# An encoder of four layers on one core: half of the second expert product in fp16 halves, the mask and the bias in fewer columns

## The reference

```
wei = jnp.einsum('bhtf,bhsf->bhts', q, k) * d ** (-0.5)
wei = jax.nn.softmax(jnp.where(tril, wei, -jnp.inf), axis=-1)
...
h = jax.nn.relu(jnp.einsum('nd,edf->enf', flat, W1) + b1[:, None, :])
eo = jnp.einsum('enf,efd->end', h, W2) + b2[:, None, :]
moe = jnp.einsum('ne,end->nd', combine, eo)
out = y + layernorm(moe.reshape(b, t, d), ln2_g, ln2_b)
```

## Time and profile before

| | before |
|---|---|
| median of the timed runs | 496.46 us (496.34 to 497.64, 3 runs) |
| the profiled execution | 499.61 us |
| its span | 497.7 us |
| mean granted clock of PE | 0.97 |
| PE busy | 458.0 us, 92% |
| ACT busy | 365.1 us, 73% |
| DVE busy | 306.5 us, 62% |
| POOL busy | 160.0 us, 32% |

### The profile page before, as it was taken

How to read it: one execution, slowest core, us unless ns; L and a number is a source line. 1 busy time by engine, 2 the same in 40 slices (tenths; PEclk the granted TensorE clock), 3 DMA queues, 4 the chain that set the end, 5 groups by cost and what they waited for, 6 DMA issues and landing times.

```text
span 497.7 us, 18273 instructions
## 1 busy us (share of the span) xinstructions
PE 458.0 (92%) x7501; PEld 380.6 (76%) x7501; DVE 306.5 (62%) x941; ACT 365.1 (73%) x906; POOL 160.0 (32%) x400
## 2 busy tenths in 40 slices
PE   6959889888889999999999999999999999999793
PEld 4736566666667888898888888898789788799693
DVE  3588988868778666487874784646634754323211
ACT  4687688788788896977779769776887676665452
POOL 6764241122224432335241144221322221432302
PEclk9778999899989999999999999999999999999997
DMA  7930000000000000000000000000000000000000
GB/s 194 380 116 3 8 3 10 9 3 3 3 3 13 3 13 3 13 3 12 3 13 3 1 3 8 10 1 3 14 3 1 1 13 4 1 12 1 12 1 12
DMA packets 7930, 11.39 MB, mean 23 GB/s; under 512 B 593, under 2 KB 7209, under 8 KB 7465
## 3 DMA queue, kind: packets, MB, share of 16 engines
q1 hardware_dynamic: 7848, 10.23, 6.3%
HBM read 9.18 MB, written 1.05 MB: 21 GB/s over the span
## 4 chain that ended last, share of the span: by engine, by line
PE 76%; DVE 10%; ACT 5%; POOL 4%; issue 3%; SPq 1%; DMA 0%; POOLq 0%; DVEq 0%; ACTq 0%
PE bk L639 23%; PE bk L629 8%; PE bk L689 6%; PE bk L691 5%; PE bk L690 5%; PE bk L615 4%; ACT w1f L806 3%; DVE negmax L1031 3%; PE bk L608 3%; PE bk L585 2%; PE bk L601 2%; PE bk L534 2%; PE bk L488 2%; PE bk L548 1%; PE bk L497 1%
## 5 line engine op out<-in xcount | busy, mean ns | idle before, releaser
L832 ACT ACTIVATE hT<-bk,pk 128x256 f32<-128x256 f32 x256 | 107.8, 479 | 41.3 <-PE bk L691 41.2
L639 PE MATMUL bk<-w2f,hT 128*128 128x128 f32 x1024 | 135.5, 276 | 1.0 <-ACT hT L832 1.0
L639 PEld LDWEIGHTS bk<-w2f,hT 128*128 128x128 f32 x1024 | 124.2, 192 | 3.9 <-ACT hT L832 1.3
L806 ACT ACTIVATE w1f<-bk 128x512 f32<-128x512 f32 (+1 forms) x192 | 98.8, 601 | 24.0 <-PE bk L615 23.4
L1031 DVE TENSOR_REDUCE negmax<-bk 128x4 f32<-128x512 f32 (+1 forms) x192 | 104.9, 612 | 15.9 <-PE bk L615 15.7
L962 DVE SCALAR_TENSOR_TENSOR acc<-bk,comb,acc 128x128 f32<-128x128 f32 x128 | 38.8, 345 | 79.9 <-PE bk L639 79.8
L689 PE MATMUL bk<-yhi,w1hi 128*128 128x256 f16 x256 | 70.2, 274 | 0.0
L691 PE MATMUL bk<-yhi,w1lo 128*128 128x256 f16 x256 | 69.8, 273 | 0.0
L690 PE MATMUL bk<-ylo,w1hi 128*128 128x256 f16 x256 | 69.8, 273 | 0.0
L629 PE MATMUL bk<-w1f,val 128*32 128x128 f32 (+1 forms) x1536 | 51.8, 278 | 2.2 <-ACT w1f L806 2.2
L615 PE MATMUL bk<-qk 32*128 32x128 f16 (+2 forms) x1536 | 46.0, 215 | 8.1 <-DVE negmax L1031 3.6
(11 more groups left out here) (150 smaller groups left out, 781.6 us busy)
## 6 DMA issues: line engine op xcount, KB each, us to landing
w1f<-in_w SPq DMA_DIRECT2D x1, 2048.0 KB, 14.9
w2f<-in_w SPq DMA_DIRECT2D x1, 2048.0 KB
pk<-in_pack SPq DMA_DIRECT2D x1, 1690.0 KB, 8.3
xin<-in_x SPq DMA_DIRECT2D x8, 128.0 KB, 2.3
out<-outb SPq DMA_DIRECT2D x8, 128.0 KB, 1.8
ctxT<-in_turned SPq DMA_DIRECT2D x8, 77.0 KB
cin<-in_ctx SPq DMA_DIRECT2D x8, 77.0 KB
hf<-in_half SPq DMA_DIRECT2D x1, 416.0 KB, 10.5
```

The costliest lines, as they stand in the source:

```text
L639: last = mm(o[:, i * D:(i + 1) * D], hT[:, k % HRING, i * T:(i + 1) * T], w2f[:, k, :], start=c == 0 and i == 0, stop=c == CH - 1, skip_gr ...
L806: act.activation(probs[0:nk, ring(n, q), :], bank(g, st, q)[0:nk, :], ACT.Exp, scale=SCALE[L]).then_inc(s_exp, 1)
L832: act.activation(hT[:, k % HRING, :], bank(g, st)[:, m * W:(m + 1) * W], ACT.Relu, bias=P("b1")[:, k:k + 1]).then_inc(s_relu, 1)
```

## The change

The constants of the mask are laid out anew, so that one product of 32 rows, 128 columns of the array and 128 columns of data writes 32 key columns of four heads for all 128 queries; four such rounds on four row groups make the mask. `combT` holds both samples' weights in 16 rows, made by one transposition, and the bias product is one with 256 columns against a block-diagonal `b2f`.

Every odd unit of the down product becomes three fp16 products of halves for each sample: hi x W2 hi, hi x W2 lo, lo x W2 hi. The halves of W2's odd units are made by four new steps "part" of lane 6 (ACT the high half, DVE the low). The halves of the relu are made by the new step "halve" behind each "moe": DVE copies `hT` into fp16, POOL subtracts (in the last job, `LATE`, DVE subtracts too). The halves lie in the place that W2's odd units had. ACT does the odd unit's relu first. `down` runs two pieces behind the up products instead of one, "moe_end" has four units, `HRING` is 6. `ORDER` and `TAKEN` are written anew throughout; the steps of the five lanes come in nearly the same sequence (on average 1.6 places away), and the pieces stand at about the same places between them.

```
-BANKS, RING, HRING = 8, 8, 4
+BANKS, RING, HRING = 8, 8, 6
...
-        return [("split", lane, n) for n in range(SPLITS)]
+        return [("split", lane, n) for n in range(SPLITS)] + [("part", lane, n) for n in range(PARTED)]
...
-        return ([("moe_start", lane)] + [("moe", lane, n) for n in range(PIECES)]
+        return ([("moe_start", lane)] + [(kind, lane, n) for n in range(PIECES) for kind in ("moe", "halve")]
...
-                    for i in range(SPS):
-                        last = pe.transpose(o[0:E1, i * T:(i + 1) * T], comb[s][:, i, :], ident)
+                    last = pe.transpose(o[0:SPS * E1, 0:T], comb[s][:].rearrange("p i e -> p (i e)"), ident)
...
-                            o = banks[q][32 * c:32 * c + 32, :].rearrange("p (t k) -> p t k", t=NT)
-                            mm(o, H(low)[rows_, :], H(spread)[rows_, x:x + T].unsqueeze(1).to_broadcast((32, NT, T)),
-                               start=True, stop=False)
+                            o = banks[q][:].rearrange("p (t k) -> p t k", t=NT)[:, :, 32 * c:32 * c + 32]
+                            mm(o, H(low)[rows_, x:x + T], H(spread)[rows_, :].unsqueeze(1).to_broadcast((32, NT, 32)),
+                               start=c == 0, stop=False)
...
             def down(j, k):
                 e, c = divmod(k, CH)
-                o = take_bank(pe, j, ("moe", MOE, 2 * e + 1), 1) if c == 0 else products(j, e)
-                pe.wait_ge(s_relu, j * UNITS + k + 1)
+                o = take_bank(pe, j, *emptied(e)) if c == 0 else products(j, e)
+                if k % 2 == 0:
+                    pe.wait_ge(s_relu, j * UNITS + k + 2)
+                    for i in range(SPS):
+                        last = mm(o[:, i * D:(i + 1) * D], hT[:, k % HRING, i * T:(i + 1) * T], w2f[:, k, :],
+                                  start=c == 0 and i == 0, stop=False, skip_group_check=True)
+                    last.then_inc(s_down, 1)
+                    return
+                u = j * ODD + k // 2
+                hi, lo = hhi(u), hlo(u)
+                pe.wait_ge(s_hhi, hi_done(u))
                 for i in range(SPS):
-                    last = mm(o[:, i * D:(i + 1) * D], hT[:, k % HRING, i * T:(i + 1) * T], w2f[:, k, :],
-                              start=c == 0 and i == 0, stop=c == CH - 1, skip_group_check=True)
+                    for w in (w2hi[:, k // 2, :], lo_of_unit(k)):
+                        mm(o[:, i * D:(i + 1) * D], hi[:, i * T:(i + 1) * T], w, start=False, stop=False,
+                           skip_group_check=True)
+                pe.wait_ge(*((s_hhi, hi_done(u) + 1) if j >= LATE else (s_hlo, u + 1)))
+                for i in range(SPS):
+                    last = mm(o[:, i * D:(i + 1) * D], lo[:, i * T:(i + 1) * T], w2hi[:, k // 2, :],
+                              start=False, stop=c == CH - 1, skip_group_check=True)
                 last.then_inc(s_down, 1)
...
-                    for i in range(SPS):
-                        last = mm(o[:, i * D:(i + 1) * D], combT[s][:, i * T:(i + 1) * T], b2f[:],
-                                  start=True, stop=True)
+                    last = mm(o[:, 0:SPS * D], combT[s][:], b2f[:], start=True, stop=True)
...
-                    if n:
-                        down(g, 2 * n - 2)
-                        down(g, 2 * n - 1)
+                    if n > 1:
+                        down(g, 2 * n - 4)
+                        down(g, 2 * n - 3)
                 elif kind == "moe_end":
-                    down(g, UNITS - 2)
-                    down(g, UNITS - 1)
+                    for k in range(UNITS - 4, UNITS):
+                        down(g, k)
...
+                elif kind == "part":
+                    act.wait_ge(s_moe, N_MOE * 16)
+                    act.activation(hi_of_w2(st[2]), odd_of_w2(st[2]), ACT.Copy).then_inc(s_w1hi, 1)
...
-                    for m in range(2):
+                    for m in (1, 0):
...
+                elif kind == "part":
+                    n = st[2]
+                    dve.wait_ge(s_w1hi, SPLITS + n + 1)
+                    dve.wait_ge(s_w1lo, SPLITS + n)
+                    dve.tensor_tensor(lo_of_w2(n), odd_of_w2(n), hi_of_w2(n), ALU.subtract).then_inc(s_w1lo, 1)
+                elif kind == "halve":
+                    k = 2 * st[2] + 1
+                    u = g * ODD + st[2]
+                    dve.wait_ge(s_relu, g * UNITS + k)
+                    dve.tensor_copy(hhi(u), hT[:, k % HRING, :]).then_inc(s_hhi, 1)
+                    if g >= LATE:
+                        dve.wait_ge(s_hhi, hi_done(u))
+                        dve.tensor_tensor(hlo(u), hT[:, k % HRING, :],
+                                          hhi(u), ALU.subtract).then_inc(s_hhi, 1)
...
+                elif kind == "halve" and g < LATE:
+                    k = 2 * st[2] + 1
+                    u = g * ODD + st[2]
+                    pool.wait_ge(s_hhi, u + 1)
+                    pool.tensor_tensor(hlo(u), hT[:, k % HRING, :], hhi(u),
+                                       ALU.subtract).then_inc(s_hlo, 1)
```

More of the change, by code:

```diff
@@ L21 @@
 SPLITS = 8
+PARTED = 4
+ODD = E1 * 2
+LATE = 7
 SPS = 2
@@ L140, in uses @@
     if kind == "moe":
-        return 1 + step[2] % 2
+        return 1 + int(step[2] > 0 and step[2] % 2 == 0)
     if step[2:] == ("B.mix",):
         return SPS
-    return int(kind in ("hop", "moe_start") or kind == "PV" and step[3] == 0)
+    return int(kind in ("hop", "moe_start", "moe_end") or kind == "PV" and step[3] == 0)
 def rounds(lane):
@@ L312, in build @@
         s_m8 = per_lane(sem, "s_m8")
-        s_xnb = per_lane(sem, "s_xnb")
-        s_xsb = per_lane(sem, "s_xsb")
+        s_bias = per_lane(sem, "s_bias")
         s_qkf = per_lane(sem, "s_qkf")
@@ L326, in build @@
         s_up, s_relu, s_down = sem("s_up"), sem("s_relu"), sem("s_down")
+        s_hhi, s_hlo = sem("s_hhi"), sem("s_hlo")
         s_accinit, s_acc = sem("s_accinit"), sem("s_acc")
@@ L373, in vacated @@
                 if slot:
-                    return s_acc, (E1 + 1) * g + step[2] // 2 + 2
+                    return s_acc, (E1 + 1) * g + step[2] // 2 + 1
                 return s_relu, 2 * (n + 1)
@@ L390, in take_bank, with emptied @@
             return bank(g, step, slot)
+        def emptied(e):
+            return (("moe", MOE, 2 * e + 2), 1) if e < E1 - 1 else (("moe_end", MOE), 0)
         def products(j, e):
-            return bank(j, ("moe", MOE, 2 * e + 1), 1)
+            return bank(j, *emptied(e))
         def ring(n, q):
@@ L406, in norm_source, with hi_done, odd_of_w2, hi_of_w2 @@
             return {"A": xin[s], "B": xs[s], "C": xs[s], "D": xs[s], "D2": on[s]}[N]
+        def hi_done(u):
+            return u + 1 + max(0, u - LATE * ODD)
+        def odd_of_w2(n):
+            return w2f[:, 8 * n:8 * n + 8, :].rearrange("p (a h x) d -> p a h x d", h=2, x=2)[:, :, :, 1, :]
+        def hi_of_w2(n):
+            return w2hi[:, 4 * n:4 * n + 4, :].rearrange("p (a h) d -> p a h d", h=2)
+        halves = w2f[:].rearrange("p u d -> p (u d)").bitcast(F16).rearrange("p (u d) -> p u d", d=2 * D)
+        def hhi(u):
+            return halves[:, 13 + 4 * (u % (HRING // 2)), :]
+        def hlo(u):
+            return halves[:, 15 + 4 * (u % (HRING // 2)), :]
+        def lo_of_w2(n):
+            if n == 0:
+                return w2lo0[:].rearrange("p (a h) d -> p a h d", h=2)
+            return halves[:, 4 * n - 3:4 * n:2, :].rearrange("p a (h d) -> p a h d", h=2)
+        def lo_of_unit(k):
+            n, m = k // 8, k % 8 // 2
+            return w2lo0[:, m, :] if n == 0 else halves[:, 4 * n - 3 + 2 * (m // 2), m % 2 * D:(m % 2 + 1) * D]
         def part_of_w1(n):
@@ L947, in hop_step @@
                     if h == "B.wo":
[L948 removed]
+                        dve.wait_ge(s_bias[s], turn(BIASED, g, 'B'))
                     dve.tensor_tensor(xs[s][:].rearrange("p i d -> p (i d)"), o[:, 0:W],
@@ L1103, in _ @@
                     pool.wait_ge(s_xn[s], norm(g, "B"))
-                    pool.tensor_tensor(xs[s][:], xs[s][:], rows_of("bo"), ALU.add).then_inc(s_xsb[s], 1)
+                    pool.tensor_tensor(xs[s][:], xs[s][:], rows_of("bo"), ALU.add).then_inc(s_bias[s], 1)
                 elif kind == "hop" and st[2] in ("B.lg", "D.lg"):
@@ L1119, in _ @@
                     pool.wait_ge(s_xn[s], norm(g, "D"))
-                    pool.tensor_tensor(xnb[s], xnD[s], rows_of("b1"), ALU.add).then_inc(s_xnb[s], 1)
+                    pool.tensor_tensor(xnb[s], xnD[s], rows_of("b1"), ALU.add).then_inc(s_bias[s], 1)
                 elif kind == "hop" and st[2] == "D.cT":
@@ L1208 @@
             "bo": a["L0_ffn_bo"]}
+    b2 = np.zeros((SPS, E1, SPS, D), f32)
+    for i in range(SPS):
+        b2[i, :, i] = a["L1_ffn_b2"]
     arrays = {
```

71 lines of the change are left out of this document (39 added, 32 removed).

## The result

| | before | after |
|---|---|---|
| median of the timed runs | 497.05 us (4 runs, 496.34 to 498.62) | 484.35 us (4 runs, 483.84 to 485.06) |
| ratio | | 0.9735 (95%: 0.9704 to 0.9765) |
| profiled execution's span | 497.7 us | 481.8 us |
| first up product of the first piece | 154.1 us | 149.1 us |
| from there to the end | 343.6 us | 332.7 us |

What follows compares the result with a forecast made beforehand. PE was taken to bound the kernel from 150 us on; -14.7 -4.6 -0.9 +1.5 +3.5 = -15.2 us from 496.5 gave 481.3 us, range 475.0 to 491.5.

Steps and rivals of the forecast that it cites:

- The bound: From 150 to 450 us PE is busy 298.0 of 300 us; before that dependences within the lanes set the pace.
- any PE time taken out comes off the end: From 150 to 450 us PE savings count in full, as long as nothing else starts to keep PE waiting.
- The down products: Odd units: six fp16 products at 0.0555 us replace 0.448 us of fp32, 128 times: -14.7 us.
- Rival B: Odd down units: weight loads not hidden in runs of six, 0.100 us a product, total 515.5 us; chance 0.07.
- The mask: Layer D score steps: four rounds take 0.222 us instead of 0.37, 32 steps: -4.6 us.
- Rival C: Mask steps gain nothing, the drain for the tiling change being paid in front: 485.9 us; chance 0.10.
- The W2 split: Four added "part" steps on ACT and DVE between 60 and 140 us: +1.5 us, bounds 0 and 2.8.
- The queue term: PE waits for halves from DVE and POOL at job ends and in the crowded stretch: +3.5 us (0 to 18).
- Rival D: No queue effect at all, the +1.5 and +3.5 us vanish: 476.3 us; chance 0.13.
- Rival A: DVE or POOL becomes the bound of the crowded stretch, giving back 8 to 14 us: about 491; chance 0.20.
- 0.8 (transpositions): Weights' transposition: one fewer per job, 0.11 us for each of 8 jobs, -0.9 us in the whole forecast.
- A first part that shifts by more than 3 us: Sign of being wrong: the part before the first piece, some 150 us, shifts over 3 us through new ORDER, TAKEN or half-clock stretches.

Runs made afterwards that it cites:

- the kernel without halves: Changed kernel without DVE's copies and the low-half subtractions; PE does the same six fp16 products from a ready tile, without waiting: 480.41 us, ratio 0.9609.
- the fp32 kernel: Changed kernel with the odd unit's down product as one fp32 product per sample, halves still made and waited for: 496.14 us, ratio 0.9923.

## Why the prediction was right, and where its terms were off

**The bound.** PE-bound from 150 us on, and slack in front of it: right. Both ways of taking PE work away moved the end, and putting it back moved it the other way: 2.4 of 3.2 us for the mask behind the first piece, 10.8 of 14.4 for the down products; and the kernel without halves keeps 14.8 of 18.4 us against the kernel before. The step that was too sure is "any PE time taken out comes off the end": a fifth to a quarter of it does not. Why is not shown. PE's recorded idle time behind the first piece hardly grows (12.0 us before, 11.8 in the kernel without halves), so what is missing doesn't lie in waits that the profile names.

**The down products.** 0.0555 us a product, taken from pairs of transpositions, holds for six in a row: 0.33 us. A piece lost 0.112 us, 128 of them 14.4 us of PE work (14.7 forecast). Rival B is out. So is the 81 ns of the Trainium skill ("TensorE: Matmul & The Clock Gate", "Back-to-back issue gap") for six pairs of a weight load and 128 columns: this trace has 55 ns each, in runs of six as in pairs, close to what the page gives as the isolated gap, 56; the measurement decides.

**The mask.** 0.13 saved a step where 0.145 was forecast, as a step up to the scores takes 0.234 us in most cases and not the 0.222 forecast; 4.2 us of PE work for 4.6, and some 3 at the end. Rival C, that the time for the change of tiling moves in front, is out: from the start of an fp32 product to the start of the mask behind it are 0.20 us in both traces (0.15 behind one of the new short products). What the forecast left in knowingly is the count: 8 of the 32 steps lie before the first piece, where the idle time of PE takes some of them.

**The W2 split.** +1.5 forecast, 0.9 or less measured, inside its bounds.

**The queue term.** +3.5 forecast, for waits at the job ends and a little in the crowded stretch. The copies and subtractions cost 3.9 us behind the first piece. Rival D, no effect at all, is out. The size was right, and so was the place: by the first up product of each job, jobs 0 to 2, which fill the crowded stretch, take 2.0 us more than without halves, and the rest about 1.9. What makes the cost was not as forecast. I looked at DVE's load, 89% of its time; by itself it turned out not to matter. The subtraction on POOL does: 1.6 to 1.8 us go with PE's wait for it, and 2.1 stay with POOL's work, where DVE's instructions are seen to take longer. The start of job 7 shows the second without any lateness in front. DVE of the changed kernel:

```profile
451.79 0.29 DVE L1108 CAST w2f<-hT 128x256 f16<-128x256 f32 x1 [3.24 <-ACT hT L889]
452.12 0.83 DVE L1111 TENSOR_TENSOR w2f<-hT,w2f 128x256 f16<-128x256 f32 x1
452.88 0.81 DVE L1108 CAST w2f<-hT 128x256 f16<-128x256 f32 x1
453.73 0.90 DVE L1111 TENSOR_TENSOR w2f<-hT,w2f 128x256 f16<-128x256 f32 x1
454.55 0.28 DVE L1108 CAST w2f<-hT 128x256 f16<-128x256 f32 x1
454.86 0.42 DVE L1111 TENSOR_TENSOR w2f<-hT,w2f 128x256 f16<-128x256 f32 x1
```

and POOL at the same time:

```profile
451.86 0.81 POOL L1215 TENSOR_TENSOR outb<-outb,base 128x256 f32<-128x256 f32 x1
452.63 0.91 POOL L1195 TENSOR_TENSOR wc<-xin,qk 128x256 f32<-128x256 f32 x1
453.62 0.72 POOL L1197 TENSOR_TENSOR base<-wc,rw 128x256 f32<-128x256 f32 x1
```

Beside POOL's instructions with two tensors from SBUF, the copy takes 0.81 instead of 0.28 and the subtraction up to 0.90 instead of 0.42; both are back to normal when POOL stops at 454.34. But lying beside each other is not enough. The first copy starts at 451.79, 0.07 ahead of POOL's addition, and takes 0.29. The second starts at 452.88, with POOL's instruction under way since 452.63, and ends at 453.69, 0.15 behind the end of that one (453.54). So it is over the whole trace: all 19 copies that start while a POOL instruction of this kind and size has over 0.16 us to go end 0.147 to 0.155 us behind it, and the 14 that start up to 0.25 us ahead of one take 0.28 to 0.31. Without POOL's subtractions only 7 copies are caught. The three DVE subtractions that are caught end 0.28 us behind POOL's. The times read as if DVE waited for POOL's instruction to end, and not as if both ran slower.

Rival A named such an effect, but as one that lengthens POOL's subtraction, and at a price of 8 to 14 us. Here it is DVE that is held longest, and all that stays with POOL's work is about 2 us. The Trainium skill, "GPSIMD Engine Reference", "Specifications", says that the two share their SBUF interfaces, with contention for VectorE's instructions in a 2-port mode or with two SBUF inputs. The trace agrees for the subtraction, which has two such inputs (0.90 against 0.42); in which mode the copy runs, no run here shows.

**What the sum missed.** Behind the first piece: 343.6 - 14.4 (down) - 3.2 (24 mask steps) - 0.8 (transpositions) = 325.2; + 3.9 (halves) = 329.1; measured 332.7. The 3.6 us left are there with no halves at all (328.8 instead of 325.2). They are the fifth of 18.4 us named under the bound, and where they lie stays open.

In front of the first piece the sum missed a gain: 5.0 us earlier instead of 1.5 later. A first part that shifts by more than 3 us is one of the prediction's own signs of being wrong, and it came. About 1 us of it is the mask and some 2 to 2.5 the clock (24 us at 1.2 GHz before 149 us in the kernel before, 14 in this one, at the 2.6 to 3.4 us for 13 that the fp32 kernel showed). The other 1.5 to 2 us stay open.

So the total is better than its parts, and that is luck. By its own terms the forecast has 15.5 us behind the first piece (14.7, 24 steps of 0.145 and 0.8, less 3.5), and 10.9 were measured; in front it has about 0.2 us of loss (1.5, less 8 mask steps and one transposition), and 5.0 of gain were measured. One error of 4.6 us and one of 5.2 the other way nearly cancel.

The medians differ by 12.7 us and the two profiled spans by 15.9. The profiled execution of the kernel before, 499.6 us, stands above its median of 497.05, and of the clock's share of 2 to 2.5 us the medians may have less: with other chips the runs of that kernel go from 496.3 to 502.6 us. How the 15.9 us of the spans are made up therefore doesn't carry over to the 12.7 of the medians in full.

## What to carry to other kernels

When TensorE is full, price a change of its work by the starts of the nearest equal instructions, however few, but don't expect to keep all of it: in this kernel three quarters to four fifths arrived at the end. If it is bought with work on VectorE and GpSimd, the load of the engine mattered less here than what stands in front in its queue (1.2 us for one late half) and whether a VectorE instruction starts while a two-input instruction of GpSimd is under way; the subtraction on GpSimd was the costlier half of the bargain though GpSimd had half its time free. And a first part without a full TensorE ran at a clock that differed from run to run: compare from the first landmark behind it.

## What the runs showed of the hardware

- Six fp16 products of 128x128 by 128 columns, each with a weight load of its own, start 0.055 us apart at a granted clock of 1.00, also directly behind fp32 products.
- 16 products on 32x32 tiles of 512 columns take 0.37 us until the next product, on all 128 columns of the array, starts; 16 on 32x128 tiles of 128 columns 0.22 to 0.24 us.
- VectorE's copy fp32 to fp16 of 128x256 in SBUF takes 0.26 to 0.30 us alone. Started while GpSimd's two-input instruction of that size runs, it ends 0.15 us behind it (up to 0.82 us in all); started just ahead of it, it takes 0.28 to 0.31. A subtraction of that size goes from 0.42 to 0.90.
- 13 us more at 1.2 instead of 2.4 GHz in the first 149 us, where TensorE is 83 to 86% busy, went with a first piece 2.6 to 3.4 us later.
- The choice of PSUM banks alone moved the kernel before by 2.3%.
